# One ScalarE operation per block for the second layer norm's scale, shift and rectifier, and a plane split one step later

## The reference

```
h = jnp.maximum(_layernorm(x, axis=-1), 0.0)
x = x + _L1_gnn_ref(h, ...)      # graph norm of gelu(...), plus h
h = jnp.maximum(_layernorm(x, axis=-1), 0.0)
x = x + _L2_gnn_ref(h, ...)      # mean over cliques, one product
h = jnp.maximum(_layernorm(x, axis=-1), 0.0)
x = x + _L3_gnn_ref(h, ...)      # sums over 206250 edges, then a GRU cell
```

## Time and profile before

| | us |
|---|---|
| median of three runs (2257.88 to 2259.93) | 2258.65 |
| the profiled execution, its own time | 2261.03 |
| its span in the trace | 2259.4 |
| TensorE busy in the span | 1973.0 (87%) |
| VectorE busy | 1539.0 (68%) |
| ScalarE busy | 1214.8 (54%) |
| GpSimd busy | 136.4 (6%) |
| share of VectorE in the chain that ended last | 6% |
| share of TensorE in that chain | 80% |

### The profile page before, as it was taken

One profiled execution on the slowest core, in us unless ns is written; L12 is line 12 of the kernel. 1 busy time (PEld: TensorE's weight loads), 2 busy tenths in 40 slices (PEclk: granted clock), 3 DMA queues, 4 the chain that ended last, 5 costly groups with the idle time before them and its releaser, 6 DMA issues.

```text
span 2259.4 us, 62757 instructions
## 1 busy us (share of the span) xinstructions
PE 1973.0 (87%) x22348; PEld 1782.8 (79%) x22393; DVE 1539.0 (68%) x3176; ACT 1214.8 (54%) x3140; POOL 136.4 (6%) x120
## 2 busy tenths in 40 slices
PE   1159999999999999999989999999986239999886
PEld 1159999999999999999987777778885228888643
DVE  8588888888888888888866666678845850000254
ACT  5756666666666666666637888889854200000232
POOL 5600000000000000000000000000012410000010
PEclk7579999999999999999999999999998569999987
DMA  8402212222222222221233334447831459888412
GB/s 228 135 32 98 96 73 96 96 80 89 96 86 83 96 93 76 96 99 70 97 135 129 124 125 137 145 144 252 318 116 46 121 175 341 300 301 300 144 54 65
DMA packets 184477, 304.09 MB, mean 135 GB/s; under 512 B 12641, under 2 KB 135958, under 8 KB 184174
## 3 DMA queue, kind: packets, MB, share of 16 engines
q1 hardware_dynamic: 180506, 290.74, 37.1%
q0 software_dynamic: 3904, 12.50, 1.9%
HBM read 202.70 MB, written 100.48 MB: 134 GB/s over the span
## 4 chain that ended last, share of the span: by engine, by line
PE 80%; DVE 6%; ACT 4%; issue 3%; DMA 3%; DVEq 2%; POOL 1%; ACTq 0%; SPq 0%; POOLq 0%
PE ps L826 24%; PE ps L926 23%; PE ps L815 10%; PE ps L809 6%; PE ps L910 6%; PE ps L896 3%; PE ps L1058 2%; PE ps L968 2%; DMA hs<-node_rows 1%; DVE hT_s L1519 1%; POOL edge_area L652 1%; ACT edge_area L1194 1%; PE ps L959 1%; PE ps L976 1%; ACT edge_area L1147 1%
## 5 line engine op out<-in xcount | busy, mean ns | idle before, releaser
L1194 ACT CAST edge_area<-ps 128x392 f16<-128x392 f32 x784 | 405.3, 517 | 393.8 <-PE ps L809 393.8
L826 PE MATMUL ps<-big,rows_area 128*128 128x128 f32 x4802 | 576.9, 277 | 0.0
L826 PEld LDWEIGHTS ps<-big,rows_area 128*128 128x128 f32 x4802 | 551.9, 192 | 0.0
L815 PE MATMUL ps<-edge_area 128*128 128x98 f16 x6272 | 416.2, 208 | 0.0
L1200 ACT COPY big<-ps 128x392 f32<-128x392 f32 x784 | 414.4, 529 | 0.4 <-PE ps L815 0.3
L1665 DVE TENSOR_TENSOR edge_area<-lo_pair,carry 128x1024 f16<-128x1024 f16 x392 | 269.4, 687 | 129.5 <-PE ps L815 126.0
L815 PEld LDWEIGHTS ps<-edge_area 128*128 128x128 f16 x6272 | 330.9, 97 | 0.0
L809 PE MATMUL ps<-edge_area 128*128 128x98 f16 x3136 | 275.6, 209 | 19.2 <-DVE edge_area L1671 11.7
L926 PE MATMUL ps<-big,rows_area 128*128 128x256 f16 (+1 forms) x2450 | 264.7, 272 | 25.7 <-DMA big<-edge_counts 25.7
L926 PEld LDWEIGHTS ps<-big,rows_area 128*128 128x128 f16 x2450 | 236.8, 98 | 53.6 <-DMA big<-edge_counts 25.9
L926 PE MATMUL ps<-big,agg 128*128 128x256 f16 (+1 forms) x2450 | 279.0, 271 | 0.0
(11 more groups left out here) (248 smaller groups left out, 1828.5 us busy)
## 6 DMA issues: line engine op xcount, KB each, us to landing
big<-edge_counts SPq DMA_DIRECT2D x336, 448.0 KB, 4.8
edge_counts<-edge_area SPq DMA_DIRECT2D x49, 1568.0 KB, 5.6
hs<-node_rows POOLq DMA_DIRECT2D x14, 448.0 KB, 4.2
edge_area<-x_stream SPq DMA_DIRECT2D x14, 448.0 KB, 3.9
node_rows<-rows_area SPq DMA_DIRECT2D x1, 3136.0 KB, 13.3
agg_s<-node_rows SPq DMA_DIRECT2D x49, 64.0 KB, 4.9
agg_s<-in_x SPq DMA_DIRECT2D x49, 64.0 KB, 1.8
x_stream<-agg_s SPq DMA_DIRECT2D x49, 64.0 KB, 1.5
```

Of the source, the lines that this page charges most:

```text
L815: last = mm(pair_of(p_weight[s % 4], c), sources_of(slot, r, c), cells_of(oh, slot, r, c), start=(c == 0 and oh is oh_whi), stop=(c == 3 a ...
L826: last = mm(p_sum, h0[:, n, :], w32[:, par, n, :], start=(n == 0), stop=(n == NB - 1))
L1194: nc.scalar.copy(store_slot[:, par, :, cols], p_count[s % 2]).then_inc(sem("count_taken"), 1)
```

## The change

The layer norm is split over two engines and two steps. VectorE now makes the moments and, with one operation of 128x7, the product `row_shift` = -mean x 1/std (`row_moments`). ScalarE then computes Relu(x x rstd + row_shift) per block, seven operations a step, straight into the `h` slot, and signals `h_rows` (its new `normalise`). VectorE makes the two planes of step i - 1 (`split_rows`) inside step i, between the clique combination and the addition of the norm's rows, after a wait for `h_rows`. The first step is taken out of the loop, and the last step's planes come after it.

```
@@ ScalarE
             act.wait_ge(sem("gain_ready"), 1)
+            def normalise(i):
+                act.wait_ge(sem("ln_scaled"), i + 2)
+                act.sem_inc(sem("passed"), 1)
+                x, h = (blocks(steps_of(t, i % 2)) for t in (row_slots[2], new_rows))
+                for b in range(SB):
+                    last = nc.scalar.activation(h[:, b, :], x[:, b, :], ACT.Relu, bias=row_shift[:, b:b + 1],
+                                                scale=rstd[:, b:b + 1])
+                last.then_inc(sem("h_rows"), 1)
+
             stage_cliques(0)
             with act.Fori(0, NS - 1) as i:
                 stage_cliques(i + 1)
                 ln_std(i)
+                normalise(i)
             ln_std(NS - 1)
+            normalise(NS - 1)
@@ VectorE
                 V.reciprocal(rstd[:], rstd[:])
                 dve.drain()
-                for b in range(SB):
-                    V.tensor_scalar(hT_s[:, b * P:(b + 1) * P], x[:, b, :], mv[:, b, 0:1], rstd[:, b:b + 1],
-                                    ALU.subtract, ALU.mult)
-                dve.drain()
-                V.tensor_scalar(h, blocks(hT_s[:]), 0.0, None, ALU.max).then_inc(sem("h_rows"), 1)
+                V.scalar_tensor_tensor(out=row_shift[:], in0=mv[:, :, 0], scalar=-1.0, in1=rstd[:], op0=ALU.mult,
+                                       op1=ALU.mult).then_inc(sem("ln_scaled"), 1)
+
+            def split_rows(i):
+
+                dve.wait_ge(sem("h_rows"), i + 1)
+                dve.sem_inc(sem("passed"), 1)
+                h = slot(new_rows, i)
                 part = [planes[:, n, bass.ds(i * SB, SB), :] for n in range(2)]
-                V.tensor_scalar(part[0], blocks(hT_s[:]), 0.0, SCALE, ALU.max, ALU.mult)
+                V.tensor_scalar(part[0], h, SCALE, None, ALU.mult)
                 dve.drain()
                 V.scalar_tensor_tensor(out=part[1], in0=h, scalar=SCALE, in1=part[0], op0=ALU.mult,
                                        op1=ALU.subtract).then_inc(sem("planes_ready3"), 1)
-                dve.drain()
@@ VectorE, the pass
-            with dve.Fori(0, NS) as i:
+            def new_x(i, first=False):
                 rows_seen(i)
                 dve.wait_ge(sem("lin3"), i + 2)
                 dve.wait_ge(sem("beyond"), i + 1)
...
                                            op0=ALU.mult, op1=ALU.add)
+                if not first:
+                    split_rows(i - 1)
                 dve.drain()
                 dve.wait_ge(sem("norm_rows"), i + 1)
                 V.tensor_tensor(n_s, n_s, z_s, ALU.add)
                 dve.drain()
                 V.tensor_tensor(slot(x2, i), slot(x2, i), n3, ALU.add).then_inc(sem("x_new"), 1)
                 dve.drain()
-                layernorm(i)
+                row_moments(i)
+
+            new_x(0, True)
+            with dve.Fori(1, NS) as i:
+                new_x(i)
+            split_rows(NS - 1)
+            dve.drain()
```

More of the change, by code:

```diff
@@ L218, in build_gnn @@
         rstd = sb("rstd", [P, SB])
+        row_shift = sb("row_shift", [P, SB])
         at_hs = hs[:].rearrange("p b d -> p (b d)")
@@ L1502, in rows_seen, with row_moments @@
                 dve.sem_inc(sem("x_seen"), 1)
-            def layernorm(i):
+            def row_moments(i):
                 x = slot(row_slots[2], i)
-                h = slot(new_rows, i)
                 for b in range(SB):
```

## The result

The changed kernel takes 2239.98 us (median of four runs, 2239.45 to 2241.93) against 2258.27 us for the kernel before in its four. The ratio is 0.9921, 95% interval 0.9907 to 0.9935: 18 us faster, where I had forecast 23.6. The forecast of 0.9896 (2235.1 / 2258.65) lies outside the interval, and the slow end of my range, 2240 us or 0.9918, lies at the measured value: as a time 2239.98 is just inside it, as a ratio 0.9921 is just beyond it. The profiled execution took 2240.14 us with a span of 2238.5.

What follows compares the result with a forecast made beforehand. VectorE's sequence was taken to set the step: six periods falling from 16.08 to 12.08 us give 24.0 us, less 0.40 in the tail, net 23.6, so 2258.65 becomes 2235.1 us; range of 8 in 10, 2228.5 to 2240.

Steps and rivals of the forecast that it cites:

- What bounds the kernel: In the layer's pass loop, VectorE's own sequence sets the step, 16.08 us; only six periods and the tail can change.
- Row_shift held to 4.75: VectorE's 128x7 operation, two SBUF inputs, is held by GpSimd's L715 and ends at 4.75 rather than 3.2 us.
- The first rival: The small 128x7 operation on VectorE is not held by GpSimd: period 11.1 us, 29.5 us less, 2229.1 us; chance 0.12.
- The Relus, 2.78 us: Seven Relus on ScalarE after row_shift take 2.78 us, by the first layer norm's rows, running from 4.85 to 7.63.
- The low bound, from L1346: Lower value for ScalarE's seven Relus: 2.15 us, as seven operations without a bias take.
- 0.1 for the semaphore: Waits between engines, row_shift to Relus and Relus to VectorE's high part: 0.1 us each.
- I take 0: VectorE's high part beside GpSimd's load L724: up to 0.25 us could come on top of 0.61; 0 was taken.
- L2046's place: VectorE's L2046 in the next step follows the last operation of a body by 0.84 us, running from 5.6 to 7.5.
- my low bound of 11.85: Shortest period in the forecast's own range, 11.85 us: faster Relus, then L2046's end at 7.5 binds.
- The tail, 0.40 us later: After the last step, storing the rows, L2059's place and the edge counts' loads come 0.40 us later.
- SyncE's load: Rival: SyncE's row stores and x loads become the bound, period 12.6 to 12.9 us, 2239.2 us; chance 0.15.
- The clock rival: TensorE's clock stays lower in layer 3's edge sums, making the kernel slower, 2270 us at 70 us low; chance 0.02.

## Why the prediction came out as it did

**What bounds the kernel** was right: the pass got shorter in every step, and what lies outside it moved by 2.4 us at most, which is within what the start of the pass varies by among the ten traces. That L1519 hid a wait for GpSimd was read from the trace only; leaving out one GpSimd operation has now shown it. That the first step keeps its time was wrong by 0.18 us, a gain.

**Row_shift held to 4.75**: measured 4.70. The value rested on one analogous row of a much larger operation, and the experiment with the moments in PSUM confirms it: the same operation, with one of its two inputs out of PSUM, is not held. "The row decides by inputs" is too short a rule, however: L1519 and the high part have one tensor input and are held too, and only the 128x1 operations with one tensor input were not. The first rival (11.1 us a step) failed as the change stands, and came true at 11.23 once the input was moved; it had counted on the hold of the high part, to 7.35 where it became 7.48.

**The Relus, 2.78 us**: 2.80. The low bound, from L1346 without a bias, was not needed. The copy behind them cost nothing, and no table load came.

**The hand-overs, "0.1 for the semaphore"**: this is the step of the prediction that failed; the mechanism was right and this term of the sum too small. I took 0.1 us twice, from no row. Measured are 0.33 (row_shift to Relu) and 0.43 (Relu to L1538), together 0.56 over the forecast, of which writing out the loops takes away 0.49. Rows on record gave a warning: from the end of L2053 at 1756.00 to ScalarE's L1346 at 1756.20 and GpSimd's L713 at 1756.30 it is 0.2 and 0.3 us, not 0.1. They do not give the whole answer, since the square root's hand-overs in the same loop are short: 0.03 us from L1514's end at 1758.44 to its start at 1758.47, and 0.03 from its end at 1758.68 to L1516 at 1758.71. Its one register row a step stands well ahead of it (first at 1740.7, the first square root at 1742.3). So a loop alone does not make a hand-over slow; register instructions behind the wait go with the slow ones.

**The high part beside GpSimd's DMA issue, "I take 0"**: it cost 0.25, the upper bound. I had argued that VectorE starts as early as GpSimd. Because the hand-overs were late, it started 0.53 us into the issue, the same offset as L1522 in the earlier trace rows (1764.27 - 1763.74), and took the same 0.86. The two errors are one: with the loops written out, it starts with the issue and takes 0.63, as I had said. In the run with the planes in the same step it started 0.40 us into the issue and took 1.00. In all three places (here, there, and L1522 in the earlier trace rows) it ended 0.43 us behind the issue's end. I read this as a hold to that end, like the one to the end of GpSimd's operations (0.47 and 0.48).

The terms add up: -0.05 (row_shift) + 0.23 + 0.02 (Relus) + 0.33 + 0.25 + 0.04 (two gaps) = 0.82 a step, which is the 12.90 of the timeline against 12.08. By the mean step, which has one step without a DMA issue in it, it is 6 x (12.84 - 12.08) = 4.6 us, and 23.6 - 4.6 = 19.0 us, as measured for the pass. The medians differ by 18.3 us and the two profiled executions by 20.9; what lies outside the pass makes up the difference in the latter, and no run explains it further.

**L2046's place, "0.84 us from the last operation of a body"**: it did not come. L2059 starts at 4.62, at the end of row_shift, and ends at 6.51, so VectorE waits 1.74 us for the Relus and not the few tenths I had named as a sign. This cost nothing, since the Relus end later, but it takes the ground from my low bound of 11.85, where L2046's end at 7.5 was to bind. Why the 0.84 us went, no run shows.

**The tail, 0.40 us later**: from L2068's end (1814.41) to L2080 it is 9.18 us, from L2053's end (1836.29) to its like 8.77: 0.41.

**SyncE's load** did not bind. The x load is issued at 1762.43, lands 3.9 us later at the median, at 16.0 on the scale above, and is wanted at 17.5. The rival's step of 12.6 to 12.9 and nearly its time (2239.2 against 2239.98) came out, but by another cause: no DMA wait stands ahead of L2059. That it has the nearest number is luck. My range for the forecast's own mechanism, up to 12.45 a step, was too narrow, since it gave "a little" to the hand-overs. The clock rival failed too: TensorE's granted clock was 0.78 over 13 us of edge sums from 1828 us in the changed kernel and 0.81 over 13 us from 1849.5 in the kernel before, and 1.00 after that in both.

## What to carry to other kernels

An operation with a wide spread of durations (here 334 ns at the median, 2119 at most) may be waiting while the profile calls it busy, as this one was; look at what GpSimd does at its start and end before costing its removal. Moving work to an idle engine pays only for what the first engine does meanwhile: here the move alone gave 0.1%, the move with the next step's work drawn over it 0.8%, and one operand in PSUM with written-out loops on top 1.35% in all, most of it by the operand (steps of 12.84, 11.23 and 10.97 us). In a chain over engines, take each hand-over from a row of the same kind, with or without address arithmetic behind its wait, since here they were two thirds of the error and brought on most of the rest.

## What the runs showed of the hardware

- A VectorE operation of 128x7 with two SBUF inputs took 0.17 us alone and 1.70 beside a GpSimd operation that had started 0.39 us before it. With one input from PSUM it took 0.17 in the same place.
- One tensor input did not always avoid it: seven tensor_scalar operations of 128x128 took 1.89 us beside no GpSimd operation, 3.56 beside one and 5.10 beside two, and one of 128x896 took 1.25 us instead of 0.63 and ended 0.47 behind the GpSimd operation beside it.
- Seven tensor_scalar operations of 128x1 with a pointer scalar, all from SBUF, took 0.205 us each beside GpSimd as well as without it, 0.94 together.
- A float32 to float16 tensor_scalar of 128x896 took 0.63 us; 0.86 when it started 0.53 us into a GpSimd DMA issue and 1.00 when it started 0.40 us into one, both times ending 0.43 us behind the issue; 0.63 when it started 0.05 us into one, which then took 1.16 us instead of 0.96; and 0.63 when it started 0.25 us ahead of one, which then took 0.97.
- The hand-over between engines took 0.12 to 0.15 us with constant addresses and 0.33 to 0.43 us in the loops where register instructions stood between the one operation's end and the other's start; the square root's, whose register row stands ahead of its wait, took 0.03 us each way in the same loop.
